# A two-layer LSTM graph network on one core: an fp32 gate table turned by PE, and the first x picked ahead of the table

## The chip, the core and the metric

The kernel runs on one core of a Trainium2 chip. The metric is the device time of one execution in microseconds (us). PE is the matrix engine, DVE, ACT and POOL are the vector, scalar and general engines, SP issues DMAs; DMA queues are also fed by ACT and POOL. PEld is PE's loading of the stationary operand.

## What is computed

x is 512 x 128, and every node has 33 neighbours (8192 edges in both directions and 512 loops, sorted by target, then cut into 512 rows of 33). Two SAGE layers each run an LSTM over the 33 neighbours of every node, then a layer norm follows, then a relational layer over the same edges (three weights, edge weights, a segment sum, relu) and a second layer norm. The part that matters here:

```python
def _lstm_last(seq, wih, whh, bih, bhh):
    b = bih + bhh
    def step(carry, x_t):
        h, c = carry
        g = x_t @ wih.T + h @ whh.T + b
        i, f, gg, o = jnp.split(g, 4, axis=-1)
        c = sigmoid(f) * c + sigmoid(i) * tanh(gg)
        h = sigmoid(o) * tanh(c)
        return ((h, c), None)
...
aggr = _lstm_last(swapaxes(x[src].reshape(n, d, c), 0, 1), wih, whh, bih, bhh)
return aggr @ wl.T + bl + x @ wr.T
```

## The kernel before

**Layout.** Channels stand on the partitions, the 512 nodes in the free dimension, in two halves of 256 (h = 0, 1). Weights and h are split into a high and a low fp16 part; a product of the recurrence is hi x hi, lo x hi and hi x lo, accumulated in fp32. The gates of a half fill two PSUM banks: bank 0 holds i and f, bank 1 holds g and o.

**Input part of a step.** x @ wih.T + b is the same for a node wherever it is a neighbour. So it is computed once for all nodes (`project`, L893, fp32, and `add_bias`, L888), split into two fp16 parts by ACT (high, L474) and DVE (low, L623) in `table_sb`, stored by SP as the gate table in DRAM (`store_chunk`, L349, four chunks of 128 nodes), and for each step POOL gathers the rows of the neighbours, four times 128 rows of 2 KB (L429), up to 5 steps ahead. `input_part` (L962) turns them into the gate banks: a row tile is the stationary operand and a scaled identity the moving one, 8 matmuls of 128 columns for each half and bank (2 gates x 2 node tiles x 2 parts), 32 in a step. For steps 0, 1, 3, 8 and 17 of each layer (`BY_ONEHOT`, the last four are `DIRECT`) nothing is gathered: `gather_x` (L910) picks x by one-hot matrices, 8 matmuls of 512 columns, ACT and DVE take its two parts (`take_x`, L511 and L639), and `gathered_part` (L918) multiplies it with wih, 24 matmuls.

**A step.** PE: input part of half 0, of half 1 (each bank after ACT has read the old gates: `if_ready`, `o_ready`), `gather_x` for the next step if that is in DIRECT (L1005), then `recurrent` of half 0 and of half 1 (24 products of 256 columns, L971; each half waits for h_hi, then for h_lo). ACT: sigmoid of i and f, tanh of g, sigmoid of o, tanh of the cell, h_hi (L485). DVE: two products, their sum, h_full (L704), h_lo (L709). Each engine has its order written out by hand. In layer 0 DVE does small work beside the steps (`beside_first_layer`), the sum of layer 1's bias at t = 9 among it.

**The start.** SP loads x turned (xT), the indices of step 0, biases, steps, indices, whh. ACT loads wih, a bias and x_nodes. PE warms up with 8 matmuls (L900), projects the table, picks x for step 0, does step 0's gates (`first_gates`) for both halves, then picks step 1's x. POOL makes the low parts of wih and whh of layer 0 (L417, L419), then waits for the table's stores and starts to gather.

**Between the layers.** sage_turned(h) (L1038) and a relu of ACT (L552) give layer 1's x, `h1T`. It is turned for the picks (L1057, fp32 transposes into gate bank 3), projected, copied and split, stored, and gathered again. `gather_x(1, 0)` waits for the first copies, since it uses work banks 0 and 1, where the table's first chunks lie. The matmuls of L1073 (h1T with the second linear weight, for the output) stand between that pick and the first gates. DVE also builds six one-hot blocks of the later stage (L692) before step 0's cell.

After 358 us the relational layer starts; the change leaves it as it is.

## Time and profile before

| | us |
|---|---|
| median of 3 runs | 490.94 (490.92 to 491.03) |
| the profiled execution | 490.78, of which its span is 488.8 |
| layer 0's recurrence, first product to last | 22.1 to 179.7 |
| layer 1's | 197.6 to 350.8 |
| PE, DVE, ACT, POOL busy | 470.8, 374.0, 337.6, 317.3 |

```profile
PE   8889999999999999999999999999998999999994
ACT  4468777877778876677888787888836455565550
DMA  4977767776777503777777767775021122122210
```

The rows show the span in 40 slices of 12.2 us, the busy share of each in tenths. Times in the trace count from the first instruction. Groups give busy time (overlaps counted once) and the mean of one; PE's matmuls overlap, so their distance, not their length, is what PE needs for one.

### The profile page before, as it was taken

To read this page: it belongs to the slowest core of one execution; us is meant where nothing else is said; L and a number is where in the kernel's file an instruction comes from. 1 tells how busy PE (TensorE), PEld (TensorE's weight loads), DVE (VectorE), ACT (ScalarE), POOL (GpSimd) and SP (SyncE) were. 2 spreads that over 40 slices of the span, in tenths; PEclk is the share of its full clock that TensorE was granted. 3 is DMA by queue.
4 is the path that set the end of the run, shared out by engine and by line. 5 is a ranking of instruction groups with operands and counts; after the bars stand their busy time and mean duration, and the time that the engine had idled before them with its cause. 6 is when DMAs were issued, how large, how long until landed. Compare 5 with 4: busy or idle time off the path is not lost.

```text
span 488.8 us, 12753 instructions
## 1 busy us (share of the span) xinstructions
PE 470.8 (96%) x5132; PEld 379.0 (78%) x5132; DVE 374.0 (77%) x985; ACT 337.6 (69%) x872; POOL 317.3 (65%) x323
## 2 busy tenths in 40 slices
PE   8889999999999999999999999999998999999994
PEld 2668888887888875888888888888776777766772
DVE  5668888888788877688888787888867966677744
ACT  4468777877778876677888787888836455565550
POOL 5577767776777403777777767774037777777760
PEclk9999999999999999999999999999999999999998
DMA  4977767776777503777777767775021122122210
GB/s 160 289 250 200 208 194 209 207 215 177 215 229 211 180 1 131 204 204 200 211 205 203 204 175 199 206 199 171 0 83 51 49 54 50 50 56 50 52 48 21
DMA packets 28546, 73.61 MB, mean 151 GB/s; under 512 B 6408, under 2 KB 10340, under 8 KB 28488
## 3 DMA queue, kind: packets, MB, share of 16 engines
q0 software_dynamic: 20672, 64.38, 45.9%
q1 hardware_dynamic: 6870, 7.77, 5.2%
q8 instruction: 40, 0.66, 0.5%
q10 hardware_dynamic: 946, 0.66, 0.4%
q14 instruction: 18, 0.15, 0.1%
HBM read 69.63 MB, written 3.16 MB: 149 GB/s over the span
## 4 chain that ended last, share of the span: by engine, by line
PE 61%; DVE 19%; ACT 10%; DMA 4%; issue 2%; POOL 1%; SPq 1%; DVEq 0%; POOLq 0%; ACTq 0%
PE gates L971 20%; PE gates L962 12%; PE work L1114 11%; PE gates L1106 10%; ACT h_hi L485 4%; DVE prod_ig L727 4%; DVE prod_fc L725 4%; DVE h_full L704 3%; PE work L910 3%; PE gates L918 3%; DVE h_lo L709 2%; DVE cell L733 2%; ACT act_if L489 2%; ACT act_if L495 2%; DMA rows<-gate_table,src_steps 2%
## 5 line engine op out<-in xcount | busy, mean ns | idle before, releaser
L429 POOL DMA_INDIRECT rows<-gate_table,src_steps x224 | 223.2, 996 | 102.4 <-issue 65.5
L971 PE MATMUL gates<-h_hi,whh_hi 128*128 128x256 f16 x512 | 126.2, 274 | 0.6
L971 PE MATMUL gates<-h_hi,whh_lo 128*128 128x256 f16 x512 | 125.7, 273 | 0.0
L443 POOL DMA_INDIRECT edge_rows<-msg_table,msg_index x86 | 87.3, 1015 | 49.3 <-DMA msg_table<-table_sb 23.4
L962 PE MATMUL gates<-ident_scaled,rows 128*128 128x128 f16 x1792 | 111.1, 219 | 3.7 <-ACT act_o L505 1.5
L962 PEld LDWEIGHTS gates<-ident_scaled,rows 128*128 128x128 f16 x1792 | 104.8, 98 | 7.1 <-ACT act_o L505 3.5
L971 PE MATMUL gates<-h_lo,whh_hi 128*128 128x256 f16 x512 | 98.2, 274 | 0.0
L485 ACT ACTIVATE h_hi<-h_full 128x256 f16<-128x256 f32 x130 | 54.2, 417 | 48.5 <-DVE h_full L704 48.5
L709 DVE TENSOR_TENSOR h_lo<-h_full,h_hi 128x256 f16<-128x256 f32 x130 | 55.4, 426 | 40.3 <-ACT h_hi L485 31.3
L489 ACT ACTIVATE act_if<-gates 128x512 f32<-128x512 f32 x112 | 66.0, 589 | 7.3 <-PE gates L971 7.3
L595 ACT ACTIVATE msg_full<-edge_rows,norm_edges 128x128 f32<-128x128 f32 x86 | 33.0, 402 | 52.7 <-DMA edge_rows<-msg_table,msg_index 52.4
L725 DVE TENSOR_TENSOR prod_fc<-act_if,cell 128x256 f32<-128x256 f32 x128 | 53.9, 421 | 13.4 <-ACT act_if L489 6.0
L1106 PE MATMUL gates<-table_lo,code_onehot 128*128 128x128 f16 x552 | 62.7, 219 | 0.0
L1106 PE MATMUL gates<-table_hi,code_onehot 128*128 128x128 f16 x552 | 62.7, 219 | 0.0
L971 PEld LDWEIGHTS gates<-h_hi,whh_hi 128*128 128x128 f16 x512 | 49.9, 97 | 12.9 <-ACT h_hi L485 2.2
L481 ACT ACTIVATE tanh_c<-cell 128x256 f32<-128x256 f32 x132 | 54.8, 415 | 1.2 <-DVE cell L733 1.1
L733 DVE TENSOR_TENSOR cell<-prod_ig,prod_fc 128x256 f32<-128x256 f32 x128 | 54.0, 422 | 2.2
L704 DVE SCALAR_TENSOR_TENSOR h_full<-act_o,tanh_c 128x256 f32<-128x256 f32 x132 | 55.3, 419 | 0.0
L1106 PEld LDWEIGHTS gates<-table_hi,code_onehot 128*128 128x128 f16 x552 | 54.0, 98 | 1.2
L1106 PEld LDWEIGHTS gates<-table_lo,code_onehot 128*128 128x128 f16 x552 | 54.0, 98 | 1.2
L971 PEld LDWEIGHTS gates<-h_hi,whh_lo 128*128 128x128 f16 x512 | 50.1, 98 | 6.1 <-issue 0.2
L727 DVE TENSOR_TENSOR prod_ig<-act_if,act_g 128x256 f32<-128x256 f32 x128 | 54.2, 423 | 0.5
(133 smaller groups left out, 627.4 us busy)
## 6 DMA issues: line engine op xcount, KB each, us to landing
rows<-gate_table,src_steps POOLq DMA_INDIRECT x224, 3.8
gate_table<-rows SPq DMA_DIRECT2D x8, 256.0 KB, 2.1
edge_rows<-msg_table,msg_index POOLq DMA_INDIRECT x86, 2.6
src_direct<-src_by_step SPq DMA_DIRECT2D x5, 256.0 KB, 5.1
code<-code_table SPq DMA_DIRECT2D x10, 128.0 KB
msg_table<-table_sb SPq DMA_DIRECT2D x4, 192.0 KB, 2.1
whhT<-turned_whh SPq DMA_DIRECT2D x2, 256.0 KB, 5.3
xT<-turned_x SPq DMA_DIRECT2D x1, 256.0 KB, 3.1
```

The costliest lines, as they stand in the source:

```text
L429: pool.indirect_dma_start(rows[:, j * K + k, :, :].rearrange("p a g -> p (a g)"), None, gate_table[l], bass.IndirectOffsetOnAxis(src_steps ...
L443: pool.indirect_dma_start(edge_rows[:, c % 2, n, :], None, msg_rows, bass.IndirectOffsetOnAxis(msg_index[:, c * NG + n:c * NG + n + 1], ax ...
L485: act.activation(h_hi[:, h, :], h_full[:, h, :], ACT.Copy).then_inc(h_hi_ready[h], 1)
L489: act.activation(act_if[:, h, :], gates[:, h, 0, :], ACT.Sigmoid, scale=1 / G_SCALE).then_inc(if_ready[h], 1)
L704: dve.scalar_tensor_tensor(h_full[:, h, :], act_o[:, h, :], H_SCALE, tanh_c[:, h, :], op0=ALU.mult, op1=ALU.mult).then_inc(h_full_ready[h], 1)
L709: dve.tensor_tensor(h_lo[:, h, :], h_full[:, h, :], h_hi[:, h, :], ALU.subtract).then_inc(h_lo_ready[h], 1)
L725: dve.tensor_tensor(prod_fc[:, h, :], act_if[:, h, HN:], cell[:, h, :], ALU.mult)
L727: dve.tensor_tensor(prod_ig[:, h, :], act_if[:, h, 0:HN], act_g[:, h, :], ALU.mult).then_inc(ig_ready[h], 1)
L733: dve.tensor_tensor(cell[:, h, :], prod_ig[:, h, :], prod_fc[:, h, :], ALU.add).then_inc(c_ready[h], 1)
L962: mm = pe.matmul(gates[:, h, b, q * HN + k * P:q * HN + (k + 1) * P], rows[:, j * K + 2 * h + k, part, gate * P:(gate + 1) * P], ident_sca ...
L971: mm = pe.matmul(gates[:, h, b, q * HN:(q + 1) * HN], w[:, gate * P:(gate + 1) * P], state[:, h, :], start=False, stop=last and q == 1, sk ...
L1106: mm = pe.matmul(gathered(c, n), code_onehot[c // 2 % 2][:, b, column:column + P], table[:, k, r * C:(r + 1) * C], start=(n % PER_BANK == ...
```

## The change

1. The gate table is fp32 (`gate_table`, `rows`), scaled by G_SCALE when ACT copies it; no low part, no DVE. `input_part` turns it with fp32 transposes against `ident`, 16 in a step in place of 32 matmuls.
2. Both bias vectors of a layer come as rows of one array and are added as two rows by the same matmul; `sum_bias` is gone.
3. `gather_x(0, 0)` comes ahead of the table's products, and in layer 1 ahead of its last two; layer 1's x is turned into banks of its own, split by half. x of step 1 is picked between step 0's halves, that of the other DIRECT steps between the halves of the input part of the step before.
4. Load order: the indices of step 0 first, x_nodes second on ACT's queue. DVE in place of POOL makes the low parts of layer 0's weights; DVE casts step 0's indices.
5. Between the layers sage_turned(1) goes ahead of all projections; L1073's matmuls go to t = 20 of layer 1; three warming matmuls become two; the four ahead of layer 0's first gates are gone.

```diff
-    gate_table = [nc.dram_tensor(f"gate_table{l}", (N, 2 * G), F16, kind="Internal").ap() for l in range(2)]
+    gate_table = [nc.dram_tensor(f"gate_table{l}", (N, G), F32, kind="Internal").ap() for l in range(2)]
...
-                      [work[:, 0, :], work[:, 1, :], work[:, 3, :], gate_bank[2]]]
+                      [gate_bank[0], gate_bank[1], gate_bank[2], work[:, 2, :]]]
+        x_bank = [gate_bank[3][:, 0:HN], work[:, 3, 0:HN]]
...
+            load_src(0)
             sp.dma_start(xT[:, :], turned_x).then_inc(x_loaded, 16)
-            load_src(0)
-            sp.dma_start(bias_in[:, 0, 0, :], bih[0].rearrange("(a g) -> a g", a=1)).then_inc(bias_loaded[0], 16)
+            sp.dma_start(bias_in[:, :, :], bias_rows).then_inc(bias_loaded, 16)
...
             act.dma_start(wihT[0][:, :], turned_wih[0]).then_inc(wih_loaded[0], 16)
-            act.dma_start(bias_in[:, 0, 1, :], bhh[0].rearrange("(a g) -> a g", a=1)).then_inc(bias_loaded[0], 16)
             act.dma_start(x_nodes[:, :, :], x.rearrange("(k p) c -> p k c", p=P)).then_inc(nodes_loaded, 16)
...
+                act.activation(table_sb[:, k, :], table_bank[l][k], ACT.Copy, scale=G_SCALE).then_inc(table_taken, 1)
+
             high_of_wih(0)
+            act.wait_ge(nodes_loaded, 16)
+            high_of_x(slice(0, K), x_nodes[:, :, :].rearrange("p k c -> p (k c)"))
+            take_x(0, 0)
+            table_part(0, 0)
             act.wait_ge(whh_loaded[0], 16)
             act.activation(whh_hi[0][:, :], whhT[0][:, :], ACT.Copy, scale=W_SCALE).then_inc(whh_hi_ready, 1)
+            for k in range(1, K):
                 table_part(0, k)
...
                     if t == 0:
+                        tanh_of_cell(0, now)
                         take_x(l, 1)
-                    high_of_h(0, now)
+                        high_of_h(0, now)
+                        i_f(1)
+                        gate_g(1, now, bias_g)
+                        gate_o(1, bias_o)
...
+                    for h in range(2):
+                        act.wait_ge(x_turned, h + 1)
+                        high_of_x(slice(2 * h, 2 * h + 2), x_bank[h])
                     act.wait_ge(table_stored, 16 * K)
                     table_part(1, 0)
                     table_part(1, 1)
-                    act.wait_ge(x_turned, 2)
-                    high_of_x(gate_bank[3])
+                    take_x(1, 0)
                     table_part(1, 2)
                     table_part(1, 3)
...
+            cast_src(0)
+            build_onehot(0)
+            low_of_x(slice(0, K), x_nodes[:, :, :].rearrange("p k c -> p (k c)"), 1)
             high_of_bias(0)
             low_of_bias(0)
...
             take_x(0, 0)
+            low_of_wih(0)
             cast_src(1)
             build_onehot(1)
+            low_of_whh(0)
...
                 for h in range(2):
+                    if h or l:
+                        pe.wait_ge(table_taken, l * K + K - 1)
                     gathered_part(l, 0, h, 0, True).then_inc(gates0[h], 1)
                     gathered_part(l, 0, h, 1, True).then_inc(gates1[h], 1)
-
+                    if h == 0:
+                        gather_x(l, 1)
+
+            gather_x(0, 0)
             pe.wait_ge(x_loaded, 16)
             pe.wait_ge(wih_loaded[0], 16)
-            for k in range(K - 1):
+            for k in range(K):
                 project(0, xT, k, first=True)
-            pe.wait_ge(bias_ready, 3)
-            for k in range(K - 1):
+                pe.wait_ge(bias_ready, 2)
                 add_bias(0, k, last=True).then_inc(projected, 1)
...
-            gather_x(0, 0)
...
-            keep_warm(work[:, 2, :], 4)
...
                     for q, gate in enumerate(BANKS[b]):
                         for k in range(2):
-                            for part in range(2):
-                                mm = pe.matmul(gates[:, h, b, q * HN + k * P:q * HN + (k + 1) * P],
-                                               rows[:, j * K + 2 * h + k, part, gate * P:(gate + 1) * P],
-                                               ident_scaled[:, :], start=(q == 0 and k == 0 and part == 0),
-                                               stop=False, skip_group_check=True)
-                    return mm
+                            pe.matmul(gates[:, h, b, q * HN + k * P:q * HN + (k + 1) * P],
+                                      rows[:, j * K + 2 * h + k, gate * P:(gate + 1) * P], ident[:, :], is_transpose=True,
+                                      start=(q == 0 and k == 0), stop=False, skip_group_check=True)
...
                             pe.wait_ge(o_ready[h], before)
                             input_part(h, 1)
-                    if t + 1 in DIRECT:
-                        gather_x(l, DIRECT.index(t + 1) + 1)
+                            if h == 0 and t + 1 in DIRECT:
+                                gather_x(l, DIRECT.index(t + 1) + 1)
...
                     if l == 1 and t == 20:
                         pe.wait_ge(residual_ready, 1)
+                        for k in range(K):
+                            pe.matmul(sum_bank[k // 2][:, k % 2 * P:(k % 2 + 1) * P], h1T[:, k * P:(k + 1) * P],
+                                      linT[:, 3, :], start=(k % 2 == 0), stop=False, skip_group_check=True)
...
-                    keep_warm(work[:, 0, :], 3)
-                    for k in range(K - 1):
-                        add_bias(1, k, first=True)
+                    pe.wait_ge(o_ready[0], T)
+                    add_bias(1, 0, first=True)
+                    add_bias(1, 1, first=True)
+                    keep_warm(work[:, 0, :], 2)
                     sage_turned(0)
...
                     pe.wait_ge(h1T_ready, 1)
                     turn_x(0)
+                    sage_turned(1)
                     project(1, h1T, 0, last=True).then_inc(projected, 1)
-                    sage_turned(1)
-                    project(1, h1T, 1, last=True).then_inc(projected, 1)
                     pe.wait_ge(h1T_ready, 2)
                     turn_x(1)
+                    project(1, h1T, 1, last=True).then_inc(projected, 1)
+                    add_bias(1, 3, first=True)
+                    gather_x(1, 0)
                     project(1, h1T, 2, last=True).then_inc(projected, 1)
                     project(1, h1T, 3, last=True).then_inc(projected, 1)
```

## Rows read from the trace of the kernel before

**Rows 1.** The page's costliest groups: form and count, busy us, mean ns, idle before.

```profile
L962 PE MATMUL gates<-ident_scaled,rows 128*128 128x128 f16 x1792 | 111.1, 219 | 3.7 <-ACT act_o L505 1.5
```

**Rows 2.** Timeline, PE, one step: start us, length us, engine, line, form, count.

```profile
170.60 1.95 PE L962 MATMUL gates<-ident_scaled,rows 128*128 128x128 f16 x32
172.48 0.28 PE L971 MATMUL gates<-h_hi,whh_hi 128*128 128x256 f16 x1
...
177.01 0.28 PE L971 MATMUL gates<-h_hi,whh_hi 128*128 128x256 f16 x1
```

**Rows 3.** Timeline, ACT and DVE, the same step.

```profile
170.80 0.38 ACT L501 ACTIVATE act_g<-gates 128x256 f32<-128x256 f32 x1
...
171.56 0.42 DVE L704 SCALAR_TENSOR_TENSOR h_full<-act_o,tanh_c 128x256 f32<-128x256 f32 x1
...
172.01 0.42 ACT L485 ACTIVATE h_hi<-h_full 128x256 f16<-128x256 f32 x1 [0.25 <-DVE h_full L704]
```

**Rows 4.** Timeline, PE, layer 0, step 2.

```profile
25.23 1.05 PE L962 MATMUL gates<-ident_scaled,rows 128*128 128x128 f16 x16 [0.31 <-issue]
27.71 1.05 PE L962 MATMUL gates<-ident_scaled,rows 128*128 128x128 f16 x16 [1.43 <-DMA rows<-gate_table,src_steps]
...
30.33 0.27 PE L971 MATMUL gates<-h_hi,whh_hi 128*128 128x256 f16 x1
```

**Rows 5.** Timeline, all engines, between the layers.

```profile
181.87 0.42 DVE L704 SCALAR_TENSOR_TENSOR h_full<-act_o,tanh_c 128x256 f32<-128x256 f32 x1
...
183.62 0.59 PE L1038 MATMUL work<-h_full,linT 128*128 128x256 f32 x2
...
184.25 0.47 ACT L552 ACTIVATE h1T<-work,bl_col 128x256 f32<-128x256 f32 x1 [1.82 <-PE work L1038]
...
188.57 1.05 PE L1073 MATMUL work<-linT,h1T 128*128 128x128 f32 x8
...
194.92 0.10 PEld L918 LDWEIGHTS gates<-xg_hi,wih_hi 128*128 128x128 f16 x1 [1.30 <-ACT xg_hi L511]
```

**Rows 6.** Timeline, PE, the fp32 transposes and a projection behind them.

```profile
182.48 0.44 PE L1057 MATMUL gates<-ident,h1T 128*128 128x128 f32 x2 [0.30 <-ACT h1T L552]
...
184.91 0.38 PE L1057 MATMUL gates<-ident,h1T 128*128 128x128 f32 x2
...
185.12 1.02 PE L893 MATMUL work<-wihT,h1T 128*128 128x512 f32 x2
```

**Rows 7.** Timeline, DVE, layer 0, t = 9.

```profile
68.08 0.67 DVE L655 TENSOR_TENSOR bias_sum<-bias_in 1x512 f32<-1x512 f32 x1
```

**Rows 8.** DMA issues: engine, count, KB, median us from issue to landing.

```profile
x_nodes<-in_x ACTq DMA_DIRECT2D x1, 256.0 KB, 5.7
```

**Rows 9.** Timeline, all engines, the start.

```profile
1.17 3.24 PE L900 MATMUL work<-zeros 128*128 128x512 f16 x8 [1.17 <-DVE zeros L668]
...
1.73 0.40 ACTq L452 DMA_DIRECT2D x_nodes<-in_x  x1
...
9.29 0.61 ACT L460 ACTIVATE x_hi<-x_nodes 128x512 f16<-128x512 f32 x1
...
9.93 0.69 DVE L633 SCALAR_TENSOR_TENSOR x_lo<-x_nodes,x_hi 128x512 f16<-128x512 f32 x1 [0.56 <-ACT x_hi L460]
```

**Rows 10.** Chain of waits in order of time: start us, us, what.

```profile
13.05 2.55 DMA gate_table<-rows
...
187.01 1.73 PE work L910 x8
```

**Rows 11.** Timeline, PE, layer 1, step 2.

```profile
200.80 1.63 PE L962 MATMUL gates<-ident_scaled,rows 128*128 128x128 f16 x21
```

**Rows 12.** Stretches: us, busy of PE, PEld, DVE, ACT, POOL; clock, DMA, GB/s.

```profile
24.40:27.80 3.40, 1.66 (x23) 1.24 (x22) 2.90 (x8) 2.75 (x9) 2.73 (x3) 1.00 0.94 327
...
481.80:485.10 3.30, 0.71 (x4) 0.40 (x4) 2.31 (x11) 0.53 (x3) 0.00 (x0) 1.00 0.00 0
485.20:488.00 2.80, 0.00 (x0) 0.00 (x0) 1.29 (x5) 0.00 (x0) 0.00 (x0) 0.50 0.31 91
```

More of the change, by code:

```diff
@@ L189, in build_program @@
         linT = sb("linT", [P, 4, C], F32)
-        rows = sb("rows", [P, SLOTS, 2, G], F16)
-        table_sb = rows[:, 0:K, :, :]
+        rows = sb("rows", [P, SLOTS, G], F32)
+        table_sb = rows[:, 0:K, :]
         h_full = sb("h_full", [P, 2, HN], F32)
@@ L215, in build_program @@
         table2_lo = sb("table2_lo", [P, K, NR * C], F16)
-        dst_onehot = [rows[:, s // 2, s % 2, :] for s in range(2 * NM)]
+        dst_onehot = [rows[:, s // 2, s % 2 * (G // 2):(s % 2 + 1) * (G // 2)].bitcast(F16) for s in range(2 * NM)]
         code = sb("code", [P, PT * P], F16)
@@ L225, in build_program @@
         whh_loaded = [sem(f"whh_loaded{l}") for l in range(2)]
-        bias_loaded = [sem(f"bias_loaded{l}") for l in range(2)]
+        bias_loaded = sem("bias_loaded")
         src_loaded = sem("src_loaded")
@@ L411, in _ @@
             pool.tensor_copy(block_iota[:, :], block_iota_i[:, :]).then_inc(iota_ready, 1)
-            for n, (scale, whole, high, high_ready, low, low_ready) in enumerate((
-                    (WX_SCALE, wihT[0], wih_hi[0], wih_hi_ready, wih_lo[0], wih_lo_ready),
-                    (W_SCALE, whhT[0], whh_hi[0], whh_hi_ready, whh_lo[0], whh_lo_ready))):
-                pool.wait_ge(high_ready, 1)
-                pool.tensor_scalar(weights_scaled[n], whole[:, :], scale, None, op0=ALU.mult).then_inc(weights_ready, 1)
-                pool.wait_ge(weights_ready, n + 1)
-                pool.tensor_tensor(low[:, :], weights_scaled[n], high[:, :], ALU.subtract).then_inc(low_ready, 1)
             pool.wait_ge(src_loaded, 16)
@@ L506, in gate_o @@
                                ).then_inc(o_ready[h], 1)
-            def take_x(l, e):
-                act.wait_ge(x_gathered[0], l * XS + e + 1)
-                act.activation(xg_hi[:, e % 2, :], work[:, 0, :], ACT.Copy).then_inc(xg_hi_ready, 1)
             act.wait_ge(cols_ready, 1)
             for l in range(2):
-                take_x(l, 0)
                 for t in range(T):
@@ L677, in _ @@
                               ).then_inc(cols_ready, 1)
-            dve.wait_ge(iota_ready, 3)
-            build_onehot(0)
-            low_of_x(0, x_nodes[:, :, :].rearrange("p k c -> p (k c)"))
-            for k in range(K):
-                table_part(0, k)
             take_x(0, 0)
+            low_of_wih(0)
             cast_src(1)
             build_onehot(1)
-            dve.wait_ge(ident_ready, 2)
-            dve.tensor_scalar(ident_scaled[:, :], ident[:, :], G_SCALE, None, op0=ALU.mult).then_inc(ident16_ready, 1)
+            low_of_whh(0)
             def build_code(batch, b):
@@ L738, in before_steps @@
                 if l == 1:
-                    table_part(1, 0)
-                    table_part(1, 1)
-                    low_of_x(1, gate_bank[3])
-                    table_part(1, 2)
-                    table_part(1, 3)
+                    for h in range(2):
+                        low_of_x(slice(2 * h, 2 * h + 2), x_bank[h], 2 + h)
                     take_x(1, 0)
@@ L1044, in _ @@
                     pe.wait_ge(whh_lo_ready, 2)
-                    pe.wait_ge(bias_ready, 6)
+                    pe.wait_ge(bias_ready, 4)
                     pe.wait_ge(wih_loaded[1], 16)
+                    pe.wait_ge(wih_hi_ready, 2)
+                    pe.wait_ge(wih_lo_ready, 2)
                     pe.wait_ge(centred_ready, 1)
-                    keep_warm(work[:, 0, :], 3)
-                    for k in range(K - 1):
-                        add_bias(1, k, first=True)
+                    pe.wait_ge(o_ready[0], T)
+                    add_bias(1, 0, first=True)
+                    add_bias(1, 1, first=True)
+                    keep_warm(work[:, 0, :], 2)
                     sage_turned(0)
                     pe.wait_ge(o_ready[1], T)
-                    add_bias(1, K - 1, first=True)
+                    add_bias(1, 2, first=True)
                     def turn_x(h):
-                        for k in (2 * h, 2 * h + 1):
-                            mm = pe.transpose(gate_bank[3][:, k * P:(k + 1) * P], h1T[:, k * P:(k + 1) * P], ident[:, :])
+                        for n in range(2):
+                            k = 2 * h + n
+                            mm = pe.transpose(x_bank[h][:, n * P:(n + 1) * P], h1T[:, k * P:(k + 1) * P], ident[:, :])
                         mm.then_inc(x_turned, 1)
@@ L1152, in lay_out @@
     laid["bias_columns"] = np.array(biases).transpose(3, 0, 1, 2)
+    laid["bias_rows"] = np.array(biases).reshape(2, 2, -1).transpose(1, 0, 2)
     for name, a in (("src", "src"), ("rel", "edge_type_3"), ("dst", "dst"), ("norm", "edge_weight")):
```

117 lines of the change are left out of this document (43 added, 74 removed).

## The prediction

> **What bounds the kernel now.** I read the shares of the page first. PE is busy 96% of the span and the group of L962, the 1792 small matmuls that the change replaces, is among its costliest [rows 1]. That invites the thought that a cheaper L962 shortens every step. So next I read one step of the recurrence in order of time, on PE, then on ACT and DVE. A step lasts 177.01 - 172.48 = 4.53 us [rows 2]. In it PE issues 32 matmuls of L962 and then 24 products of L971. The 32 start at 170.60 and the last of them, 219 ns long, ends at 172.55 [rows 1, 2], so 31 distances fill 1.95 - 0.22 = 1.73 us: 55.8 ns each, 1.79 us for 32. The first product could follow at 172.39, but it starts at 172.48.
>
> What holds it is the other chain. The products of half 1 end, tanh of gate g runs from 170.80, then its product on DVE, h_full of half 0 from 171.56, and its fp16 part h_hi from 172.01 for 0.42 us, to 172.43 [rows 3]. The first product needs h_hi and starts 0.05 us after it. From the first L962 to the first product there are 1.88 us, of which PE needs 1.79. **A plain step is thus bound by the way from products through ACT and DVE back to the products**, and L962 lies in its shadow with 0.09 us to spare. The high share of PE hides this, since a matmul's row runs to its end and not to the start of the next.
>
> PE itself is the bound only where more stands between two sets of products: the steps that also pick an x (L910), those beside DIRECT steps, and t = 20. The rest of the time is lost where the chain of waits leaves the loop: at the start, where step 2 of layer 0 waits for its gathered rows [rows 4], and at the change of layers [rows 5].
>
> **Transposes in place of pairs of fp16 matmuls.** 32 matmuls become 16 fp32 transposes of 128 columns. The kernel before has such transposes: a pair of L1057 starts at 184.91 and the next instruction behind it at 185.12, so 0.21 us for two, 0.107 each; after a wait the pair starts at 182.48 and ends at 182.92, which puts its second start at 182.65, 0.17 behind the first [rows 6]. I take 0.109 (the width of a 256-column fp16 product on the same line of time; 0.105 to 0.11 is what the rounding leaves). 16 x 0.109 = 1.74 us instead of 1.79. Bounds: 0.107 and, if each paid the 0.17 of a pair after a wait, 16 x 0.17 = 2.7 us. In the 44 or so plain steps the gain of 0.05 is worth nothing, since 1.88 us is given by the chain; it becomes a loss above 1.88 / 16 = 0.117 us. In the steps bound by PE (t = 2, 7 and 16 of each layer, and t = 20) it counts: some 5 x 0.04 = **-0.2 us** (t = 2 is counted below). Bytes of a gathered row stay 2 KB, so the gathers are as before.
>
> **The bias of layer 1.** Its sum, 0.67 us of DVE at 68.08 between h_lo and prod_fc, goes [rows 7]. In a plain step about 0.3 us of that place is idle, so **-0.35 us** (0 to -0.67). Its high and low parts stay.
>
> **The start.** Now the picking of the first x stands ahead of the table on PE, so the table, its stores and the gathers wait for x_nodes. Before, x_nodes was issued at 1.73 and took 5.7 us to land, at 7.43 [rows 8, 9]; now its issue comes one small load earlier, about 0.5 us, and it lands at 6.9 (bounds 6.3 and 7.43). The high part takes 0.61, the low part 0.69 [rows 9]: 7.5 and 8.2. The eight pick matmuls take 1.73 us [rows 10], 7.6 to 9.3. Then four chunks of the table: 2 passes of 0.43 (two L893 span 1.02 [rows 6], the second of them 0.59) and a bias of 0.22, 1.07 each: to 13.6. The last copy is done 0.2 + 0.6 later, at 14.4, and needs no DVE part. Before, the last store went out at 13.05 and took 2.55 us [rows 10]; now it is issued at 14.4 and takes 2.1 to 2.55, 16.5 to 17.0 instead of 15.60. **The gathered rows come 0.9 us later**, at 26.1 (half 0) and 28.6 (half 1) in place of 25.23 and 27.71 [rows 4]. PE's own way is shorter (step 1's products some 1.5 us earlier), which is worth nothing here. But step 3's pick (1.73 us), which stood behind half 1's rows, now stands between the halves, where PE waits for rows anyway: 26.1 + 0.87 + 1.73 = 28.7, half 1's transposes to 29.6, and the products of step 2 start there and not at 30.33 [rows 4]. **-0.7 us**, from -1.3 (x_nodes at 6.3) to +0.2 (7.43 and the slow store). POOL no longer splits the first weights (DVE does, behind the picks, where nobody waits yet).
>
> **The change of layers.** Before, sage_turned(1), whose h_full was ready at 182.29, stood behind project(1, 0): it started at 183.62 and relu of half 1 at 184.25 [rows 5]. Now it goes first: at 182.76, relu at 183.45, 0.8 us earlier. x is turned into two banks of their own and split by half, so its parts are there at 185.4 and the pick starts right behind the second projection, 185.35, not at 186.84. Its eight matmuls end at 187.1, the last two projections (0.86 each) at 188.8; the third chunk is copied at 188.75, which the first gates wait for. The four fp32 matmuls of L1073, 0.89 us at 188.57, go to t = 20. First gates half 0 to 190.2, pick of step 1 to 191.9, half 1 to 193.2, and step 1's own L918 start there, where before they started at 194.92 after 1.30 us idle [rows 5]. That is -1.75; I take **-1.6** for some waits not seen, -0.9 to -1.8. The table's last chunk is ready 1.2 us later than before (189.6), but the rows of step 2 then land near 200.0 and are used at 201.0, behind the pick. Moved to t = 20, a step bound by PE, the L1073 cost 0.89 - 0.04: **+0.85 us**.
>
> **Step 2 of layer 1.** PE's 21 last L962 take 1.63 us where 21 x 0.056 + 0.16 = 1.33 would do [rows 11]: 0.3 us wait for act_o of half 1. With the pick ahead of half 1, it is there in time: **-0.3 us**, and later steps 7 and 16 gain nothing by the new place.
>
> **Sum**, against the profiled execution's own 490.78 us: -0.2 - 0.35 - 0.7 - 1.6 + 0.85 - 0.3 = -2.3, so 488.5; the median of the runs is 0.16 above that execution, so **488.6 us**. By the ends of the terms, 487.4 to 490.3.
>
> **The rivals.** (a) **PE's clock falls in the new idle stretches of the start.** Nothing runs on PE between the warm-up, which ends at 4.4 [rows 9], and the pick at 7.6, and again between step 1's products (23.2) and the rows at 26.1. For it: at the end of the kernel PE was busy 0.71 of 3.30 us and the clock of the next stretch is 0.50, so 1.2 GHz. Against: with 1.66 of 3.40 us busy it stayed at 1.00 [rows 12]. Here a stretch of that length would hold 0.3 to 1 us of work. Before the rise, at the start, eight 512-column matmuls took 3.24 us [rows 9], about 0.4 each; picks and the first projections at that pace cost 1.7 us more on the way to the table. The second fall costs as much again in part. One fall gives 490.3 (489.6 to 491.5), which is mostly no change.
>
> (b) **Slower: the fp32 weight load shows.** If the load before each transpose isn't hidden beside fp16 products, the distance goes from 0.109 towards the 0.17 seen after a wait. It decides from 0.117 on; at 0.14 a plain step has 2.24 in place of 1.88 us, + 0.36 x 48, 506 us. A milder form, 0.06 for each of four waits in a step, gives 1.98, + 0.1 x 48, 493. Against it stands the pair behind work of another kind at 0.107 [rows 6].
>
> (c) **PE counts after all**: if the 0.09 us ahead of the first product were PE's own and not the wait for h_hi, each of 46 steps would gain 0.14: 482. The end of h_hi 0.05 us before speaks against it.
>
> (d) **The clock falls within the steps.** The rows show 1.00 while fp16 matmuls fill PE, and say nothing of transposes in that share; without them 24 x 0.109 = 2.6 of 4.5 us stay, more than the 1.66 of 3.40 at which it held [rows 12]. Should it fall, 24 products cost 2.6 us more in each of 62 steps: 650 us. The Trainium skill (TensorE: Matmul & The Clock Gate, Part 4: PE-mode transpose) has this as a rule: transposes don't count as busy PE. By that rule alone the new input parts add nothing to keep the clock; no row here shows it at work.
>
> (e) **The reordering gives little**: x_nodes late, the switch held by ACT's queue. 490.3.
>
> **How the numbers follow.** Forecast 0.44; (a) 0.31; (b) 0.08; (c) 0.04; (d) 0.02; (e) 0.11. The range 487.4 to 491.3 takes in the forecast, (a) nearly whole and (e), some 0.84. About 0.2% (0.98 us) is what a measurement of this kernel can tell from no change, so faster is below 489.96 and slower above 491.92. Faster: all of the forecast, a third of (a), (c), a third of (e): 0.61. Same: the rest of (a) and (e): 0.29. Slower: (b), (d): 0.10.
>
> **What would show it.** L962's successor at 0.109 us, and 1.88 us still between the first transpose and the first product; the steps of 4.53 unchanged. A granted clock of 1.00 from 4 to 30 us says that (a) did not happen. Products of step 2 at 29.6, step 1's L918 of layer 1 some 1.6 us after 193 less what the start gave. The forecast is wrong if the plain step changes at all, or if x_nodes lands after 7.4.

## The result and the profile after

The changed kernel takes **496.88 us** (median, 492.85 to 497.18) where the kernel before takes 490.93: ratio **1.0099**, 95% interval 1.0058 to 1.014. The forecast was 488.6 us with a range to 491.3, so both the time and the sign were wrong. The profiled execution is the shortest one, 492.85 us (span 491.0); the others lie between 494.7 and 497.18. That step between executions turns out to be part of the answer.

I read the recurrence first. The page's group of the transposes in the changed kernel (busy us, mean ns, idle before), then its PE timeline around one plain step:

```profile
L934 PE MATMUL gates<-ident,rows 128*128 128x128 f32 x896 | 109.9, 273 | 5.7 <-issue 3.6
...
171.02 0.28 PE L941 MATMUL gates<-h_hi,whh_hi 128*128 128x256 f16 x1
173.67 1.91 PE L934 MATMUL gates<-ident,rows 128*128 128x128 f32 x16
175.56 0.28 PE L941 MATMUL gates<-h_hi,whh_hi 128*128 128x256 f16 x1
```

Half the instructions, the same step: 175.56 - 171.02 = 4.54 us, and 175.56 - 173.67 = 1.89 from the first transpose to the first product, as in [rows 2]. Over 36 steps that only fetch, the mean is 4.541 us, in the kernel before 4.540. So the time was not lost here.

The chain of waits of the changed kernel at the start (start us, us, what) shows where it was:

```profile
1.18 6.53 DMA x_nodes<-in_x
...
8.51 3.29 PE work L885 x8
11.80 0.86 PE gates L868 x2
12.65 0.32 PE gates L863
12.97 1.05 PE gates L868 x2
...
17.76 2.01 DMA gate_table<-rows
...
20.64 6.16 DMA rows<-gate_table,src_steps
26.80 3.58 issue
30.39 1.06 PE gates L934 x8
31.45 1.73 PE work L885 x8
33.18 0.87 PE gates L934 x8
34.05 0.67 PE gates L941 x6
```

x_nodes lands at 7.71, the eight picks (L885) take 3.29 us, each later chunk of the table 1.05 + 0.32 = 1.37 us, the last store lands at 19.77, and the rows of step 2's half 0 are there at 30.39 instead of 25.23 [rows 4]. "issue 3.58" is PE waiting for the second tile of that half. Step 2's products start at 33.89 us, 3.56 later than the 30.33 of [rows 4].

The stretches of the same execution (us, busy of PE, PEld, DVE, ACT, POOL, granted clock, DMA share, GB/s):

```profile
4.50:8.50 4.00, 0.23 (x1) 0.02 (x1) 1.67 (x6) 1.26 (x2) 0.00 (x0) 0.93 1.03 353
8.50:11.40 2.90, 2.89 (x7) 1.03 (x8) 1.76 (x4) 0.60 (x1) 0.00 (x0) 0.50 0.06 23
...
26.70:30.40 3.70, 0.10 (x2) 0.04 (x1) 2.95 (x8) 2.66 (x8) 2.79 (x4) 1.00 1.03 321
```

PE was idle for nearly the whole 4 us ahead of the picks, and then worked 2.9 us at 0.50, which is 1.2 GHz. That is rival (a), its first fall. In a second idle stretch, 26.7 to 30.4, the clock held in this execution.

The rest went as forecast. From layer 0's last products to those of step 1 of layer 1 it takes 18.97 us for 20.55 (-1.58), the next step 6.09 for 6.43 (-0.33), the one ahead of t = 20 of layer 1 7.03 for 6.22 (+0.81), t = 9 and 10 of layer 0 together 0.51 less. Sum with the start's +3.56 and 0.18 in step 3 and some small ones: +2.0, and 490.78 + 2.0 = 492.8, the profiled 492.85.

### The profile page after: what moved, and what is told of

Read it like the earlier page. It is cut to its first block, busy times and chain, and to the rows that moved or that the text cites. A ratio compares the mean times of both kernels' runs of the same rounds, so it can differ in the third digit from the quotient of the medians.

```text
span 491.0 us, 10938 instructions
## 1 busy us (share of the span) xinstructions
PE 471.0 (96%) x4231; PEld 373.6 (76%) x4231; DVE 368.8 (75%) x978; ACT 338.2 (69%) x872; POOL 311.5 (63%) x319
## 4 chain that ended last, share of the span: by engine, by line
PE 53%; DVE 26%; ACT 12%; DMA 4%; issue 3%; POOL 1%; SPq 0%; ACTq 0%; DVEq 0%; POOLq 0%
PE gates L941 14%; PE work L1084 11%; PE gates L1076 10%; PE gates L934 8%; ACT h_hi L472 6%; DVE prod_ig L706 6%; DVE prod_fc L704 6%; DVE h_full L683 5%; PE work L885 4%; DVE h_lo L688 3%; DVE cell L712 3%; ACT act_if L476 3%; PE gates L893 3%; DMA x_nodes<-in_x 1%; DMA rows<-gate_table,src_steps 1%
## 5 line engine op out<-in xcount | busy, mean ns | idle before, releaser
L934 PE MATMUL gates<-ident,rows 128*128 128x128 f32 x896 | 109.9, 273 | 5.7 <-issue 3.6
L934 PEld LDWEIGHTS gates<-ident,rows 128*128 128x128 f32 x896 | 99.7, 140 | 9.9 <-ACT act_o L492 4.0
L941 PEld LDWEIGHTS gates<-h_hi,whh_hi 128*128 128x128 f16 x512 | 49.9, 97 | 16.3 <-ACT h_hi L472 10.6
L941 PEld LDWEIGHTS gates<-h_lo,whh_hi 128*128 128x128 f16 x512 | 45.3, 97 | 11.7
```

Source lines behind the costliest of these rows:

```text
L934: pe.matmul(gates[:, h, b, q * HN + k * P:q * HN + (k + 1) * P], rows[:, j * K + 2 * h + k, gate * P:(gate + 1) * P], ident[:, :], is_tran ...
L941: mm = pe.matmul(gates[:, h, b, q * HN:(q + 1) * HN], w[:, gate * P:(gate + 1) * P], state[:, h, :], start=False, stop=last and q == 1, sk ...
```

## The experiments

Two of the chips used treat all versions of this kernel alike in one way: from step 2 of layer 0 on, the rows come much later, and the kernel before takes 647 or 630 us there. Of the runs there I use the first 20 us and the steps that no gather delays. All of them but warm_load_bias were repeated on chips where the kernel before takes 491 us (labels that end in _2). after_2, warm_both_2, table_first_2 and transposes_only ran on one where its median is 491.35 (489.56 to 494.54), the other four on one where it is 491.01 (490.18 to 491.77).

**The clock, held by filling both idle stretches.** The changed kernel, with 24 warming matmuls in place of 8 ahead of the first pick and 12 ahead of step 2's rows. The added zero matmuls do no work of the computation.

```
-            keep_warm(work[:, 0, :], WARM)
+            keep_warm(work[:, 0, :], 24)
...
                         j = turn % DEEP
+                        if l == 0 and t == 2:
+                            keep_warm(work[:, 2, :], 12)
```

> The changed kernel unaltered, once more, since the chip of the first call ran every kernel some 150 us longer, with each step of the recurrence near 6 us. Theory S (all the loss is at the start): 492.8 or 497 us, step 2's products at 33.9 or near 38 us, plain steps 4.53 to 4.55. Rival R (the loss of the runs near 497 lies in the steps): some plain steps above 4.6 us.

> As warm_both, on another chip: PE is kept busy with zeros in both idle stretches of the start. If the fallen clock costs what the first profile shows, 490.5 to 491.5 us and one level; if the late rows are due to order and loads alone, 492.5 to 493; Rival R: two levels as before, since the steps are untouched.

Measured: the changed kernel again 496.06 us (492.35 to 497.35; ratio 1.0066, 1.0037 to 1.0096); with both stretches filled 492.09 (490.74 to 492.74; 1.0015, 0.9998 to 1.0033), between the two times expected. The granted clock of warm_both_2 is 1.00 from 4.4 to 485 us. So **4.0 us of the median are the clock**; the ratios, with their wider intervals, differ by only 0.0051 or 2.5 us, the two profiled executions by 5.1. after_2's plain steps keep the distances of the first trace, with 4.54 us in most, so rival R is out. Its profiled execution, 496.12 us, shows the second fall. The stretch of step 2:

```profile
29.70:36.50 6.80, 5.88 (x20) 3.72 (x21) 1.57 (x4) 1.21 (x3) 5.28 (x6) 0.50 0.93 308
```

and its chain, whose last four rows are to be held against the last four above:

```profile
8.84 3.57 PE work L885 x8
...
30.62 1.94 PE gates L934 x8
32.56 3.41 PE work L885 x8
35.97 1.21 PE gates L934 x8
37.19 0.67 PE gates L941 x6
```

Transposes, pick and transposes take 6.57 us instead of 3.66, so this fall costs 2.9 us. They start 0.23 later too, and the products stand at 37.19 for 34.05: +3.14, nearly all of the 3.27 between the two profiled executions. In warm_both_2 the first picks take 1.89 us for 3.57, and the same three pieces 3.66. But with the clock held the kernel is still 0.7 us above the kernel before beside it, where the forecast had it 2.3 below: **some 3 us of the miss have nothing to do with the clock**. warm_both_2's trace shows 2.2 of them on the way to step 2's rows, which start at 28.34 and not at 26.1: 1.0 is x_nodes' landing (7.92 for 6.9), 1.0 the four chunks (5.3 for 4.3), the rest small.

**The order of the start.** Three things at once: table ahead of the picks, xT's load ahead of the broadcast of step 0's indices, the four biases behind the four projections; transposes and the new change of layers stay.

```
-            load_src(0)
             sp.dma_start(xT[:, :], turned_x).then_inc(x_loaded, 16)
+            load_src(0)
...
-            gather_x(0, 0)
             pe.wait_ge(x_loaded, 16)
             pe.wait_ge(wih_loaded[0], 16)
             for k in range(K):
                 project(0, xT, k, first=True)
-                pe.wait_ge(bias_ready, 2)
+            pe.wait_ge(bias_ready, 2)
+            for k in range(K):
                 add_bias(0, k, last=True).then_inc(projected, 1)
+            gather_x(0, 0)
```

(ScalarE's copies of the table go ahead of its copy of the pick, and the bias parts ahead of the one-hot on DVE, in the same way.)

> As table_first, on another chip: the table's products ahead of the first pick, xT loaded first, biases behind all four projections. Theory S: step 2's products at 26.5 to 28 us, 485 to 487.5 us, one level of times. Rival R: 495 or more and two levels.

Measured: **486.92 us**, ratio 0.9894 (0.9858 to 0.9929), as expected; step 2's products are at 28.32, 0.3 later than the latest expected. Its chain:

```profile
1.19 3.59 PE work L874 x8
4.78 2.77 PE gates L867 x4
7.55 1.72 PE work L867 x4
...
10.24 1.85 PE work L884 x8
...
23.42 1.40 issue
24.82 1.06 PE gates L934 x8
...
28.48 0.67 PE gates L941 x6
```

xT is there at 3.78, so the projections follow the warm-up at once and fill the time in which the other order waits for x_nodes. The last bias ends near 10.2 instead of 17.1, the stores land at 14.64 instead of 19.77, and PE waits 1.40 us for step 2's rows, not 3.6. The clock doesn't fall again once it is up. But in this execution it was up late: the first four projection passes take 2.77 us and the next four 1.72. The rows come only 0.4 us ahead of the kernel before (24.82 for 25.23), though the last store landed 1.0 ahead of it.

**The load order alone, and the bias alone.**

```
-            load_src(0)
             sp.dma_start(xT[:, :], turned_x).then_inc(x_loaded, 16)
+            load_src(0)
```

> The changed kernel with nothing but xT's load issued ahead of the broadcast of step 0's indices, no zero matmuls added, on a chip where the kernel before takes about 491 us. Theory (late loads and the fallen clock are two separate terms): everything up to step 2 comes 0.7 to 0.9 us earlier, TensorE still idles about 4 us ahead of the first pick and again ahead of step 2's rows, the clock falls as before in at least one of the two; ratio 1.005 beside after_2's 1.0066, 495. Rival (the late loads were what let the clock fall): no fall, step 2's products near 31, ratio 0.9995 as expected of warm_load_2.

> The changed kernel with both idle stretches of the start filled by zero matmuls (24 at the beginning, 12 ahead of step 2; they do no work of the computation), as the earlier run warm_both, and now the load of xT issued ahead of the broadcast of step 0's indices. Theory (the late loads are a term of their own): xT lands near 3.9 us instead of 6.9, x_nodes near 7.0 instead of 7.7, so picks, table chunks, stores and rows all come 0.7 us earlier; step 2's products at 31.1 us where the run with the old load order had 31.8, and a median about 0.7 us below it: 491.4 beside a kernel before of 491.3. Rival (only the order of picks and table matters): the picks wait for the one-hot of step 0's indices anyway, step 2's products stay at 31.8 and the median at 492.1.

> The kernel of warm_load (changed kernel, both idle stretches of the start filled with zero matmuls, xT's load issued ahead of the broadcast of step 0's indices) on a chip where the kernel before takes about 491 us. The other chip showed the table's stores and step 1's products 0.85 and 0.92 us earlier than with the new load order (21.89 where warm_both had 22.81). Theory (the start's delay is handed on whole): step 2's products 0.9 us ahead of warm_both_2's 31.84, at about 30.9, and a ratio to the kernel before of 0.9995 to 1.000 where warm_both_2 had 1.0015. Rival (the first gather and its loads take up the gain): step 2's products at 31.8, ratio 1.0015.

xt_first_2: 494.88 us, ratio 1.0089 (1.0063 to 1.0114), not to be told from after_2's 1.0066. xT lands at 3.88 and x_nodes at 6.94 (in after_2 7.14 and 8.04), and step 2's products come 0.5 us ahead of the first trace (33.37 for 33.89). Yet PE idles ahead of the pick and the clock is down by 7.7 all the same, so the rival is out:

```profile
4.50:7.70 3.20, 0.00 (x0) 0.00 (x0) 1.55 (x6) 0.84 (x2) 0.00 (x0) 0.96 1.03 317
7.70:11.10 3.40, 3.32 (x9) 1.38 (x10) 1.79 (x5) 0.60 (x1) 0.00 (x0) 0.53 0.15 57
```

warm_load had step 1's products at 21.89 us for 22.74 in warm_both on another chip of that kind, as the theory said. warm_load_2 had them at 22.35 for 22.81 (its warm-up ends at 8.42 and holds up the picks), but its ratio is 1.0015, the same as warm_both_2's: the rival. The chain of warm_load_2 and, for the same place, that of warm_both_2:

```profile
27.73 1.03 issue
28.76 1.06 PE gates L934 x8
```

```profile
28.18 0.16 issue
28.34 1.06 PE gates L934 x8
```

Its stores were issued 0.45 us earlier and its rows came 0.42 us later. **Here an earlier table gave nothing.** This is one pair of traces: from the last store's landing to the second tile of rows it takes 9.7 us in warm_both_2, 10.6 in warm_load_2, and 9.5 to 10.6 in the others whose loads run beside the gathers, without relation to how early the stores land.

> The kernel of warm_load, and the four bias matmuls of the first table behind its four projections instead of each behind its own. Theory (each switch between fp32 projection and fp16 bias costs TensorE about 0.3 us): the last projected chunk is complete 0.6 to 1.2 us earlier than in warm_load; the table copies then stand close behind one another on ScalarE (0.6 us each), so that the last store is issued 0.4 to 0.9 us earlier, step 2's products are at 30.2 to 30.7 us and the median is about 490.8. Rival (the gaps are the ends of the projections and stay wherever the bias stands): within 0.2 us of warm_load everywhere.

Half right. PE's timeline of warm_load (bias behind each projection), then of warm_load_bias:

```profile
9.52 1.02 PE L868 MATMUL gates<-wihT,xT 128*128 128x512 f32 x2
...
14.59 0.39 PE L863 MATMUL work<-bias_parts,ones 34*128 34x512 f16 x1
```

```profile
10.04 1.88 PE L868 MATMUL gates<-wihT,xT 128*128 128x512 f32 x4
...
14.01 0.59 PE L863 MATMUL work<-bias_parts,ones 34*128 34x512 f16 x2
...
15.48 1.09 ACT L454 ACTIVATE rows<-work 128x512 f32<-128x512 f32 x2
```

From the first projection to the last bias's start it takes 14.59 - 9.52 = 5.07 us with the bias in between and, the second of the last pair following 0.22 us behind the first, 14.23 - 10.04 = 4.19 without: the switches cost PE **0.9 us in all**. But no chunk is ready before all are projected, so ScalarE copies them late: the last copy ends 6.53 us after the first projection, where it was 6.10. For the stores this version is 0.4 us worse. It would be about even without ScalarE's copy of whh, which fell into a wait before and now takes 0.5 us between the first two copies of the table. In table_first's order that copy comes later, so the gain should stand there; it was not measured by itself.

**What slows the first gather.** table_first, and the loads that nothing needs before step 3 held back:

```
             for k in range(K):
                 store_chunk(0, k)
+            for k in range(K):
+                sp.wait_ge(rows_in[k], 16)
             sp.dma_start(lin_in[:, :, :], turned_lin).then_inc(lin_loaded, 16)
```

> The kernel of loads_later (table_first, and the loads that nothing needs before step 3 held back until the first four gathers of rows have landed) on a chip where the kernel before takes about 491 us. Theory (the loads beside it slow the first gather): rows of step 2 land at 21 to 25 us instead of 23.4 to 27.0, step 2's products at 26.5 instead of 28.3, ratio to the kernel before 0.985 where table_first_2 had 0.9894. Rival (the gathers queued behind it set its time): rows and products as in table_first_2, ratio 0.989 or, if a held load is late, above.

Measured: **485.39 us**, ratio 0.9893 (0.9875 to 0.9911), the shortest time of all. Time from issue to landing of the first four gathers, table_first_2 and then loads_later_2:

```profile
DMA to landing us min/median/max: 7.6/7.8/8.0
```

```profile
DMA to landing us min/median/max: 3.5/3.6/4.4
```

So the loads beside it more than double the gather's time. The same trace shows it once more: three gathers issued between 22.9 and 25.8 us, beside the loads now let go, take at least as long as table_first_2's:

```profile
DMA to landing us min/median/max: 8.1/8.4/8.9
```

Step 2's products come at 26.02 us instead of 28.32, and its PE then waits for nothing between step 1's products and step 2's transposes:

```profile
20.09 2.62 PE gates L943 x24
22.71 0.87 PE gates L936 x8
...
26.18 0.67 PE gates L943 x6
```

Not all 2.3 us are the gathers'. In this execution the clock was up earlier, and PE's timeline has the first four projection passes at

```profile
4.35 1.88 PE L869 MATMUL gates<-wihT,xT 128*128 128x512 f32 x4
```

where table_first_2 needed 2.98, so its last store went out at 10.39 and not at 11.72, and step 1's products start 0.7 us earlier. From there to step 2's products it takes 6.09 us for 7.68: **1.6 us are the gathers'**. The ratio is the rival's 0.989 and not the 0.985 of the theory, and the same as table_first_2's within the intervals. So the effect on the gathers is shown by the traces, a gain in the median is not.

**The transposes alone**: the kernel before with nothing but the fp32 table and its transposes, DVE's low part of the table gone.

```
-                            for part in range(2):
-                                mm = pe.matmul(..., rows[:, j * K + 2 * h + k, part, gate * P:(gate + 1) * P],
-                                               ident_scaled[:, :], ...)
+                            mm = pe.matmul(..., rows[:, j * K + 2 * h + k, gate * P:(gate + 1) * P], ident[:, :],
+                                           is_transpose=True, ...)
```

> The kernel before with one part of the change alone: fp32 table and transposes, no DVE part of the table; order, loads, picks and biases as before. My theory: plain steps stay at 4.53 to 4.55 us, 1.88 from the first transpose to the first product, since h_hi holds them; steps with a pick lose 0.04; the start wins 1 to 1.5 us and the change of layers 0.3 to 0.8 by the missing DVE parts: 488.7 to 489.8 us. If PE's own time set the plain step, 0.09 to 0.14 us less in each of some 46 steps: 483 to 485. If transposes let the clock fall, over 495.

Measured: 489.74 us, ratio 0.9961 (0.9943 to 0.998), within the expected range; plain steps 4.541 us. The parts are not all as expected: the change of layers takes 20.55 us as before, so the missing DVE parts gave nothing there, and from step 2's products to the end it is 0.4 us shorter, for the steps that PE bounds. The other 1.2 of the median's 1.6 us must then lie in the start. The last store is issued 1.0 us earlier (12.06 for 13.05), since it no longer waits for the low parts on DVE, but no trace shows what that gives at step 2. For the profiled execution, 492.55 us, had one fall of the clock, with the old order, and its products of step 2 at 32.48 for 30.33:

```profile
26.50:29.00 2.50, 0.83 (x8) 0.86 (x9) 0.71 (x2) 0.42 (x1) 1.89 (x3) 1.00 0.85 265
29.00:32.50 3.50, 3.50 (x12) 1.29 (x10) 0.00 (x0) 0.60 (x1) 2.67 (x3) 0.51 0.77 214
```

**PE's slack in a plain step.** table_first and, in the fetched steps, extra zero matmuls of 128 columns that do no work of the computation:

```
+                    if t not in DIRECT and (l == 0 or t < 20):
+                        for _ in range((6, 2)[l]):
+                            pe.matmul(work[:, 3, 0:P], zeros16[:, 0:P], zeros16[:, 0:P], start=True, stop=True)
                     for h in range(2):

                         recurrent(h, l * (T - h) + t)
```

> The kernel of step_plus (table_first and 6 more zero matmuls of 128 columns in each fetched step of layer 0, 2 in those of layer 1 up to step 19) on a chip where the kernel before takes about 491 us. On the other chip its undisturbed steps took 4.702 us in layer 0 (0.16 more) and 4.505 us in layer 1 (0.03 less). Theory (slack of TensorE's gap used up between two and six): 4.70 for every plain step of layer 0, 4.51 for those of layer 1, so 24 times +0.16 and some 13 times -0.03 on table_first_2's 486.9: 490.4. Rival (the chip decides, and TensorE's sum counts here): 4.88 and 4.65, about 498.

```profile
154.80 0.50 PE L996 MATMUL work<-zeros 128*128 128x128 f16 x6
155.14 0.27 PE L941 MATMUL gates<-h_hi,whh_hi 128*128 128x256 f16 x1
...
159.84 0.27 PE L941 MATMUL gates<-h_hi,whh_hi 128*128 128x256 f16 x1
```

The first product's start in two steps that follow each other: layer 0's plain steps take 159.84 - 155.14 = 4.70 us (+0.16), those of layer 1 4.53 as without extras; 491.30 us in all (490.4 expected, 498 by the rival), ratio 1.0006. Six extras add 0.34 us of PE work and 0.16 of time: the slack is 0.18 us a step. PE is not the bound, and it is close to it.

**The first runs, on the other two chips.**

> The changed kernel once more, unaltered. In its first profile every plain step of the recurrence had the distances of before (4.53 to 4.55 us), and the loss was all at the start: step 2's products at 33.89 us and not 30.33, with the clock at half from 7.96 to 11.38. But most of its timed runs lie 4 us above that one, near 497. Theory S (start alone): in those runs the clock falls again in the idle time of PE ahead of step 2's rows (26.7 to 30.4 us), and a profile of such a run shows step 2's products near 38 us and all later steps as before. Rival R (recurrence): the transposes do not keep the clock up, and a profile of such a run shows some steps well above 4.55 us at half clock.

> The changed kernel with 16 more matmuls of zeros in the first warm-up and 12 ahead of step 2's wait for its rows. They do no work of the computation. Theory S with the clock as its cause: the granted clock stays 1.00 from 4 to 400 us, the eight picks take 1.73 us and not 3.1, the two levels of times become one, and the run takes 490.5 to 491.5 us (492.85 less 1.7). If the late rows were due to the order and the loads alone, 492.5 to 493.

> The changed kernel with the start of before in one respect: the table's products stand ahead of the first pick on all engines, and xT is loaded first; the four biases follow the four projections. Everything else of the change stays. Theory S: the stores go out by 10 to 11 us, the gathered rows come 3 us earlier than even before the change, step 2's products start at 26.5 to 28 us, and the run takes 485 to 487.5 us with no second level of times. Rival R (the loss comes from the transposes and the clock in the steps): 495 or more, two levels of times as in the changed kernel.

> The changed kernel with one load moved: xT ahead of the indices of step 0, as before the change. In the changed kernel wih and the indices land at 6.11 and 5.92 us, in the kernel before wih and xT at 4.03 and 3.86. If the broadcast of the indices as the first load is what holds the others up, wih lands near 4.0 again and x_nodes near 7.0 rather than 7.71, and the start comes 0.5 to 0.7 us earlier. If it is chance of the memory, nothing changes: 492.9 or the upper level near 497.

> The kernel of table_first with extra TensorE work in the fetched steps, behind the input transposes and ahead of the recurrent products: 6 zero matmuls of 128 columns (0.05 to 0.06 us each) in those of layer 0, and 2 in those of layer 1 up to step 19; they do no work of the computation and go to a bank that nothing else uses then. Theory (a plain step is a ring through TensorE, ScalarE and VectorE of 4.54 us in which the input part lies in a gap of TensorE with about 0.15 us to spare): the 0.11 us of layer 1's two matmuls cost nothing (4.54 stays), the 0.34 us of layer 0's six cost 0.15 to 0.25 us a step (4.70 to 4.80), about 6 us in all over 27 steps: 493. Rival 1 (TensorE's total work sets the step): +0.34 in layer 0 and +0.11 in layer 1, 4.88 and 4.65, about 498. Rival 2 (large slack): both at 4.54 and the median at 487.

> The kernel of table_first (transposes of a float32 table and the new change of layers, with the load order, the table ahead of the picks and the bias behind the projections in the first layer), and the loads that nothing needs before step 3 held back until the first four gathers of rows have landed. Theory (the first gather is slowed by the loads beside it: its rows landed from 23.4 to 27.0 us there, 7.9 us after its first issue): rows land near 21 to 25 us, step 2's products at 26.5 instead of 28.3, and the median at about 485.2. Rival (the gather's own descriptors set its time): rows as late as before, 487, or above that where a held load comes too late for step 8's pick.

Beside the kernel before at 647.35 us: changed kernel 635.84 (0.9832, 0.9778 to 0.9885), warm_both 637.85 (0.9849), table_first 631.55 (0.9765), xt_first 634.40 (0.9761). Beside 630.30 on the second chip: warm_load 624.83 (0.9922), warm_load_bias 618.92 (0.9836), step_plus 621.11 (0.9872), loads_later 619.65 (0.9836). No expected time was met. In after_again step 2's products come 25.0 us after step 1's (9.9 in the usual run), and the largest wait of PE's weight loads is at the transposes, without a releaser:

```profile
PEld gates L934 <- issue: 42.5, 38, 8.7
```

What could be read there agrees with the runs above: step 1's products at 24.05 us in the changed kernel, 23.40 with xT first, 22.74 with the clock held, 20.22 with the table first; and the steps that wait for no rows take 4.53 us, 4.70 with six extras, 4.51 with two. Why rows come late on these chips, and why the changed kernel is 1.7% faster there and 1% slower elsewhere, was not settled: the landings of the gathers are not in those traces.

## Why the prediction was wrong

**Right**: what bounds a step. Transposes 0.109 us apart, 1.89 us to the first product, 4.541 us a step; step_plus_2 puts the slack at 0.18 us; the rows had given 0.09, and 0.14 with the 0.05 that the transposes save. Rivals (b), (c) and (d) are out. On (d), the rule named from the Trainium skill (TensorE: Matmul & The Clock Gate, Part 4: PE-mode transpose) changed nothing here: with the transposes among products the granted clock is 1.00 from 34 to 481 us. Whether transposes alone hold it is open: in transposes_only it fell behind a stretch whose only work, 0.83 us, was transposes.

**Right within 0.05 us each**: the change of layers (-1.58 for -1.6), L1073's move (+0.81 for +0.85), step 2 of layer 1 (-0.33 for -0.3). The last is near its limit: in warm_both_2 and warm_load_2 the rows land late enough (202.25 for transposes that start at 202.34) that this step takes 6.40 and 6.53 us, for 6.43 before. The bias sum was worth 0.5 for 0.35. Of rival (e), the late x_nodes came true and the held-up change of layers did not.

**Wrong: the start**, +3.56 us for -0.7 in the profiled execution, and 2.9 more where the clock falls twice. By the steps of that part:

- x_nodes at 6.9, at the latest 7.43: it landed at 7.71, outside the bounds and past the 7.4 that the prediction had named as the sign of its being wrong. I had counted only one issue less ahead of it. The broadcast of step 0's indices, now first, goes ahead of the matrices on the DMA engines: xT lands at 6.86 here and x_nodes at 7.71; with xT first (xt_first_2) they land at 3.88 and 6.94, which is the forecast's 6.9. A load's landing can't be moved by its issue time alone.
- Eight picks at 1.73 us: 3.29, the clock at 1.2 GHz. The forecast had put this term at nothing. Rival (a) had it at 1.7 with the first projections, and came within 0.2 of it.
- Four chunks at 1.07: 1.37 each. I added 0.43 + 0.43 + 0.22 from rows in which like follows like; each change between fp32 projection and fp16 bias costs more. With these three, the last copy ended at 17.7, not 14.4.
- Rows of half 0 came 10.6 us behind the last store's landing (19.77 to 30.39), where I had kept the 9.6 of before (15.60 to 25.23): the first four gathers take 6.2 to 8.2 us here. So 30.39 instead of 26.1, of which 3.3 are the stores' (19.77 for 16.5) and 1.0 the gathers'. Loads beside a gather can do this (loads_later_2), and here the gathers issued behind the loads, from 33.5 us on, take 3.6 to 4.0. But loads ran beside the gathers before the change too, so what made these 1.0 us longer is not shown; in warm_both_2 they were only 0.1 longer.
- Step 3's pick between the halves: from half 0's rows to the products it takes 3.50 us as forecast. But half 1's rows were there at 31.92, so only 0.6 of its 1.73 us lay in a wait, not all of it.

**Two steps of the prediction failed: the sum of the start, and the clock.** The sum took x_nodes' landing and the chunks from rows of the old order and came out 2.2 us short even with the clock held (warm_both_2: 28.34 for 26.1). The clock was put at full speed throughout, and its price in rival (a) stopped at 1.7 and "as much again in part"; the larger share of the miss lies here. The first picks at half clock cost 1.7 us in after_2 (3.57 for 1.89), the second fall 2.9, since the transposes and the whole pick behind the idle stretch run at half the clock and stand on the path. So (a) named the right mechanism, but on a start that was too short and with a second fall too cheap: 496 was measured, not 490.3 to 491.5. And the second fall had the weaker evidence against it: [rows 12] had 1.66 of 3.40 us busy, while here the stretch holds 0.10 of 3.70.

Not settled: why the second fall comes in some executions and not in others (xt_first_2's profiled one had PE busy 0.00 of 3.30 us from 26.5 to 29.8 at a clock of 1.00, and kept it); and what each of late loads and switches is worth in the total, since taking one away alone (warm_load_2, warm_load_bias) shifted the wait to the next. table_first_2 mends order, loads and bias together, so its gain isn't divided either.

## What to carry to other kernels

Work moved ahead of a long path must have its own input as early as the path's, or the whole path takes over that input's wait; here projections that needed 3.9 us of loading were put behind a pick that needed 7.7. Price each idle stretch that a new order leaves on TensorE with the clock's fall, and put all that runs behind it at half speed into the price. A transfer's duration holds only for the company in which it was measured: the same gather took 3.6 us with the loads held back and 7.8 beside them.

## What was not expected of the hardware

- An fp32 transpose of 128 columns: 0.109 us apart, as long as a 256-column fp16 product; its weight load of 140 ns stays hidden.
- The gap between an fp32 projection and an fp16 matmul beside it: 0.53 us from the projection's second pass to the bias and 0.32 from the bias to the next, for 0.43 and 0.22 among their own kind.
- A clock that is shown can be wrong before its first record: in after_2 the stretches from 1 to 12.6 us read 1.00, while eight picks take 3.57 us, as at 1.2 GHz. There durations decide. The eight warming matmuls stand 0.43 us apart to the last, as at 1.2 GHz, so in this execution the clock may not have risen at all before the picks.
- The clock fell in the kernel with only the transposes changed as well, after a stretch with 0.83 of 2.50 us busy. That order has PE idle for 2.10 us ahead of half 1's rows where the kernel before had 1.43. The kernel before may fall too: of its 25 executions on that chip the five above 493 us have a mean clock of 0.992 to 0.995, the others, up to 492.59, 0.995 to 0.998. No trace of the five shows where.
